# Attention step: the image columns and the image corner of the weights turned by TensorE, the image part of the weighted sum as one 153-column product a group, set-up fills in another order

## What is computed

```python
attn = jnp.einsum('bhnd,bhmd->bhnm', q, k) * attn_scale
attn, a_scale = fq_act(attn)              # to 8 bits, one scale for all
attn = log_int_softmax(attn, a_scale)     # integer exp, sum, ratio, then 0 or a power of two
out = jnp.einsum('bhnm,bhmd->bhnd', attn, v)
```

## Time and profile before

| | us |
|---|---|
| median of 3 runs | 1046.6 (1045.37 to 1047.09) |
| the profiled execution, its own time | 1041.93 |
| its span, first to last instruction | 1040.1 |
| attention, of that span | about 355 to 775 |
| mean granted TensorE clock | 0.841 of 2.4 GHz |

### The profile page before, as it was taken

How to read it: one execution, slowest core, us unless ns; L and a number is a source line. 1 busy time by engine, 2 the same in 40 slices (tenths; PEclk the granted TensorE clock), 3 DMA queues, 4 the chain that set the end, 5 groups by cost and what they waited for, 6 DMA issues and landing times. The chain is left out here.

```text
span 1040.1 us, 22682 instructions
## 1 busy us (share of the span) xinstructions
PE 709.4 (68%) x5955; PEld 482.6 (46%) x5956; DVE 883.8 (85%) x2422; ACT 711.7 (68%) x1376; POOL 168.9 (16%) x274
## 2 busy tenths in 40 slices
PE   3872396747888366666776676666645385999997
PEld 3552144424555233433443343343323254989896
DVE  5898986888888889999999999999978864666766
ACT  0254364957888699888888989899955294445453
POOL 5851500006555000000000000000003530000000
PEclk9995598988999687788777778878756597999999
DMA  8000000001111111111111111111012004355452
GB/s 255 3 2 0 0 1 1 0 0 38 37 37 37 33 29 25 24 23 23 23 29 24 24 23 25 24 23 24 13 62 105 18 1 151 126 193 203 154 199 89
DMA packets 84272, 54.71 MB, mean 53 GB/s; under 512 B 53705, under 2 KB 83177, under 8 KB 83977
## 3 DMA queue, kind: packets, MB, share of 16 engines
q1 hardware_dynamic: 83208, 54.11, 17.1%
q0 software_dynamic: 1024, 0.13, 0.2%
HBM read 11.90 MB, written 3.76 MB: 15 GB/s over the span
## 5 line engine op out<-in xcount | busy, mean ns | idle before, releaser
L1358 DVE SCALAR_TENSOR_TENSOR expo<-expo,con,pow 128x153 f32<-128x153 f32 x480 | 146.1, 376 | 0.8 <-ACT expo L1267 0.8
L1141 PE MATMUL at_rem<-word,ident_half 128*128 128x459 f16 x160 | 66.0, 412 | 102.9 <-ACT expo L1267 102.1
L1267 ACT ACTIVATE expo<-at_rem,con 128x459 f32<-128x459 f32 x160 | 95.2, 639 | 14.2 <-PE at_rem L1142 13.5
L953 DVE TENSOR_REDUCE rs_ends<-rs_banks 128x770 f32 (+1 forms) x96 | 91.3, 960 | 14.5 <-PE rs_banks L924 12.8
L873 ACT ACTIVATE rs_banks<-rs_banks 128x770 f32<-128x770 f32 x96 | 76.2, 798 | 25.3 <-PE rs_banks L916 24.0
L1223 ACT ACTIVATE word<-at_banks 128x459 uint8<-128x459 f32 x160 | 80.9, 560 | 10.7 <-PE at_banks L779 10.6
L1401 DVE CUSTOM_DVE_ANT_0 weight_top<-weight_top,line 128x2448 uint16<-128x2448 uint16 x64 | 86.2, 1346 | 2.1 <-ACT line L1259 2.1
L1141 PEld LDWEIGHTS at_rem<-word,ident_half 128*128 128x128 f16 x160 | 15.7, 98 | 152.9 <-ACT expo L1267 148.3
L1259 ACT ACTIVATE line<-weight_top 128x1224 f32<-128x1224 f32 x64 | 74.0, 1158 | 15.2 <-DVE weight_top L1386 15.0
L774 PE MATMUL at_banks<-pick,row_top 128*128 128x459 bf16 x160 | 73.4, 459 | 11.0 <-ACT word L1223 4.0
L1907 ACT ACTIVATE qk<-e_p,b1s 128x153 f32<-128x153 f32 x192 | 58.7, 391 | 29.8 <-PE e_p L1868 28.5
(11 more groups left out here) (390 smaller groups left out, 2089.8 us busy)
## 6 DMA issues: line engine op xcount, KB each, us to landing
qk<-vt SPq DMA_DIRECT2D x64, 384.0 KB, 3.1
rs_kb<-qk SPq DMA_DIRECT2D x128, 28.7 KB, 1.9
kb<-qk SPq DMA_DIRECT2D x128, 28.7 KB, 1.9
patches<-in_patches SPq DMA_DIRECT2D x4, 768.0 KB, 10.0
vi<-vt SPq DMA_DIRECT2D x32, 96.0 KB, 2.0
out<-vi SPq DMA_DIRECT2D x32, 96.0 KB, 1.8
pj_w<-in_w SPq DMA_DIRECT2D x1, 2304.0 KB, 8.4
qb<-qk SPq DMA_DIRECT2D x128, 6.0 KB, 1.8
```

The costliest lines, as they stand in the source:

```text
L953: v.tensor_reduce(ends[:, :, n, 5 * b:5 * b + 5], banks[:, slot(u, b), :, 0:5 * W].rearrange("p i (t n) -> p i t n", n=W), AX, ALU.max).th ...
L1141: pe.matmul(out, identh[:, :], bank(word, b).bitcast(F16), start=True, stop=False)
L1267: act.activation(bank(ex, b), rem[:, (u + b) % 2, 0:3 * N], ACT.Square, scale=2.0 ** 24, bias=c(5)).then_inc(sq_done, 1)
L1358: ins = v.scalar_tensor_tensor(ex[:, t, :], ex[:, t, :], c(7), pw[:, t, :].bitcast(BF16), ALU.add, ALU.mult, accum_out=tot[:, t:t + 1])
```

## The change

The vector transpose of the corner and the two ACT gathers (`p_image`, `p_both`) go. Group 2 on PE now is: three 128 x 128 transposes of planes 12 to 14 as before; 12 transposes that each turn one text plane's 32 image columns straight into its 32 partitions of the output (L1168); 12 products with a 32 x 32 piece of the identity, that turn the corner block by block (L1174, written as f32 into spare columns of the same PSUM buffer). ACT evicts the turned image rows and corner side by side into a single piece `imT` of 153 columns a group of heads, so that `weighted` needs one product for each instead of two, and `pT_all` shrinks from 2316 to 2295 columns. Both halves of L1386 (L1392 in the new numbering) and the image shares on ACT now wait for all three groups of PE. At the start of the stage the fills of `row_top` and `zero` go from DVE to POOL, ahead of POOL's fill of `word`; ACT no longer waits for all set-up before it copies the first rows, and PE waits for it only before `remainder`.

```diff
-        pi, pk = sb("p_image", [P, H, 32], BF16), sb("p_both", [P, HT, 32], BF16)
-        pall = sb("pT_all", [P, H * N + HT * (P + 32)], BF16)
+        pall = sb("pT_all", [P, RT * N], BF16)
...
+        imT = pall[:, H * N:RT * N].rearrange("p (t n) -> p t n", n=N)
...
             def _(pool):
+                pool.memset(row_top[:, :, :], 0.0).then_inc(words_set, 1)
+                pool.memset(zero[:, :], 0.0).then_inc(words_set, 1)
                 pool.memset(word[:, :, :], WORD).then_inc(words_set, 1)
...
                 def remainder(n, u, which):
+                    if first(n, 1):
+                        pe.wait_ge(set_up, 3)
...
                 def turn(n, u, which):
-                        if g == GROUPS - 1:
-                            pe.wait_ge(pi_done, n + 1)
...
-                            src = high[:, t, 0:NT] if t < RT else pi[:, 4 * (t - RT):4 * (t - RT) + 4, :].rearrange("p j n -> p (j n)")
-                            mm = pe.transpose(pT[:, slot, j * P:(j + 1) * P], src, identb[:, :])
+                            if t < RT:
+                                mm = pe.transpose(pT[:, slot, j * P:(j + 1) * P], high[:, t, 0:NT], identb[:, :])
+                            else:
+                                for q in range(4):
+                                    mm = pe.transpose(pT[32 * q:32 * q + 32, slot, j * P:(j + 1) * P], high[:, 4 * (t - RT) + q, IW:N], identb[:, :])
+                        if g == GROUPS - 1:
+                            for t in range(HT):
+                                for j in range(4):
+                                    r = slice(32 * j, 32 * j + 32)
+                                    mm = pe.matmul(corner_at(slot)[r, 32 * t:32 * t + 32], high[:, H + t, IW:N], identb[:, r], start=True, stop=True, skip_group_check=True)
                         mm.then_inc(tr_done, 1)
...
-                        pe.matmul(po[p:p + 64, q:q + NT], lhs, piT[:, t, :], start=False, stop=False, skip_group_check=True)
-                        pe.matmul(po[p:p + 64, q + NT:q + N], lhs, pjT[:, t, ID:32], start=False, stop=False, skip_group_check=True)
+                        pe.matmul(po[p:p + 64, q:q + N], lhs, imT[:, t, :], start=False, stop=False, skip_group_check=True)
...
                 turn_tops(0)
-                pe.wait_ge(set_up, 4)
...
-                def corner(n):
-                    if not first(n, 1):
-                        act.wait_ge(tr_done, n * GROUPS)
-                        act.wait_ge(pk_done, n)
-                    act.wait_ge(i_done, n * 2 + 2)
-                    act.activation(pi[:, :, :].bitcast(I16), high[:, 0:H, IW:N].bitcast(I16), ACT.Copy).then_inc(pi_done, 1)
-                    rank(pk[:, :, :], high[:, H:RT, IW:N]).then_inc(pj_index, 1)
...
-                            rank(piT[:, :, :], slot[:, 3 * P:6 * P].rearrange("p (t n) -> p t n", n=P)).then_inc(ev_done, 1)
+                            rank(imT[:, :, 0:NT], slot[:, 3 * P:6 * P].rearrange("p (t n) -> p t n", n=P))
+                            rank(imT[:, :, NT:N], corner_high((u + g) % 2)[:, :, ID:32]).then_inc(ev_done, 1)
...
-                act.wait_ge(words_set, 1)
-                act.wait_ge(set_up, 4)
                 per_step = act.alloc_register("per_step")
                 act.load(per_step, con[0:1, 0:1].bitcast(I32))
+                act.wait_ge(words_set, 1)
                 keep_tops(0)
+                act.wait_ge(words_set, 3)
+                act.wait_ge(set_up, 3)
...
-                v.memset(row_top[:, :, :], 0.0).then_inc(set_up, 1)
-                v.memset(zero[:, :], 0.0).then_inc(set_up, 1)
+                v.sem_inc(set_up, 1)
...
-                            v.wait_ge(pj_index, nb)
+                            v.wait_ge(tr_done, nb * GROUPS)
                         for h, half in enumerate(halves):
-                            if not first(nb, 1):
-                                v.wait_ge(tr_done, nb * GROUPS - 1 + h)
...
-                        v.wait_ge(pj_index, nj + 1)
-                        if not first(nj, 1):
-                            v.wait_ge(pv_done, nj)
-                        v.transpose(pjT.rearrange("p t n -> p (t n)"), pk[:, :, :].rearrange("p t n -> p (t n)")).then_inc(pk_done, 1)
                         v.wait_ge(ev_done, nj * GROUPS + GROUPS)
-                        v.wait_ge(pk_done, nj + 1)
```

More of the change, by code:

```diff
@@ L1019, in attention @@
         vbs, zero = sb("v_image_row", [P, 2, HT * 4 * HD], BF16), sb("zero_column", [P, 2], BF16)
-        pi, pk = sb("p_image", [P, H, 32], BF16), sb("p_both", [P, HT, 32], BF16)
-        pall = sb("pT_all", [P, H * N + HT * (P + 32)], BF16)
+        pall = sb("pT_all", [P, RT * N], BF16)
         ptT = pall[:, 0:H * N].rearrange("p (h n) -> p h n", n=N)
-        piT = pall[:, H * N:H * N + HT * P].rearrange("p (t n) -> p t n", n=P)
-        pjT = pall[:, H * N + HT * P:H * N + HT * (P + 32)].rearrange("p (t n) -> p t n", n=32)
+        imT = pall[:, H * N:RT * N].rearrange("p (t n) -> p t n", n=N)
         high = top[:, :, :].bitcast(BF16).rearrange("p w (n two) -> p w n two", two=2)[:, :, :, 1]
@@ L1029, in attention, with corner_at, corner_high @@
         pT, po = k.ps("at_pT", [P, 2, 1024], BF16, st), k.ps("at_out", [P, 512], F32, st)
+        def corner_at(slot):
+            return pT[:, slot, 6 * P:6 * P + 2 * HT * 32].bitcast(F32)
+        def corner_high(slot):
+            return pT[:, slot, 6 * P:6 * P + 2 * HT * 32].rearrange("p (t n two) -> p t n two", t=HT, two=2)[:, :, :, 1]
         sem = lambda *names: (k.sem("at_" + y) for y in names)
@@ L1034, in attention @@
         ends_done = k.sem("at_ends_done")
-        pi_done, pj_index, pk_done, pj_done, tr_done, ev_done, pv_done, out_done = sem(
-            "pi_done", "pj_index", "pk_done", "pj_done", "tr_done", "ev_done", "pv_done", "out_done")
+        pj_done, tr_done, ev_done, pv_done, out_done = sem(
+            "pj_done", "tr_done", "ev_done", "pv_done", "out_done")
         pj_loaded, a_done = k.sem("pj_loaded"), k.sem("at_a_done")
@@ L1167, in weighted @@
                             pe.wait_ge(out_done, half)
+                        else:
+                            pe.wait_ge(words_set, 2)
                         pe.matmul(po[:, 0:1], identb[:, :], zero[:, 0:1], start=True, stop=False, skip_group_check=True)
@@ L1248, in both_shares @@
                     if not first(n, 1):
-                        act.wait_ge(pj_index, n)
+                        act.wait_ge(tr_done, n * GROUPS)
                     for t in range(H, RT):
@@ L1282, in body @@
                     if last is not None:
-                        corner(last[0])
                         ranks(last[0], last[1])
```

## The result

| | before | after |
|---|---|---|
| median | 1045.37 (7 runs) | 1042.02 (7 runs) |
| ratio, 95% interval | | 0.9963 [0.9951, 0.9976] |
| the profiled execution, its own time | 1041.93 | 1042.02 |
| attention in it, barrier to barrier | 420.01 | 414.92 |
| everything else in its span | 620.11 | 625.30 |

The account below looks back on a forecast made before the run. DVE's own order was taken to set the pace, with ACT's second `line` a floor just under it. Loop 2.3 - 1.3 = 1.0, start 1.9, end 0.6: 3.5 off 1046.6 gives 1043.1 on the median's scale; range 1038.5 to 1049.

Parts of the forecast that it names:

- The floor: DVE's second addition waits for ACT's second `line`, so it starts no earlier than 4.91 after the shares; 4.99 before.
- 28 steps x 0.08 = 2.3: Attention loop on DVE: dropping the 0.38 transpose gains 0.08 a step in 28 of 32 steps, 2.3 us.
- PE's group 2, the minus 1.3: Loop: group 2 takes 0.83 at 2.4 GHz, about 1.25 at 1.2; in 9 slow steps ACT is 0.15 late, 1.3 back.
- The rule on small matmuls: PE's group 2: some 60 cycles of overhead per matmul would make it 1.15 and cost the sum some 0.5; weighed, not taken.
- the 0.28 of the sum: PE's group 2: time taken for the 24 small products, in rounds of four, 0.18 for transposes and 0.10 for corner products.
- The start: 1.9: Start of attention: evictions finish earlier, DVE is last, POOL's added fills cost 0.35; `octave` moves from 364.84 to 362.93.
- The end: 0.6: Last step: first addition keeps 0.25 of the 0.38, last rounding about 0.3 earlier, fewer products 0.05; together 0.6.
- The whole 0.38 counts: Rival, loop on DVE: all 0.38 of the transpose is gained in 28 steps, 13.1 in all, 1033.5; chance 5%.
- The gain is eaten: Rival: low-clock delays in half the steps, or PE or POOL at the start, leave -1.5 to +1.5, say 1045.8; chance 20%.
- One by one: Rival: PE's small products run serially, group 2 is 0.8 longer at 2.4 GHz, 13 us lost in the loop, 1054.8; chance 13%.
- Its turning point: In the serial-products rival: the change turns slower once group 2 on PE takes more than about 1.5.
- What would show it: Profile signs: DVE idle 0.3 before second addition, step 12.48, DVE below 98%; wrong if ACT's third eviction waits over 0.5 for PE.

Follow-up runs that it names:

- no_floor: Changed kernel with one square instead of two between ACT's two `line`s, and the maximum of finished output ahead of DVE's first addition; 1030.03 (5 runs), ratio 0.9847.
- two_transposes: Changed kernel with two idle 128x96 block transposes per step put on DVE, each into a piece of its own; one run, 1041.38.
- one_piece: Changed kernel with 24 more small PE products, all into the first 32 partitions, ahead of the proper ones that overwrite them; one run, 1054.19.

## Why the prediction was right, and where not

**The floor.** Forecast: the second addition 4.91 after the start of the shares, 0.08 gained, not 0.38. Measured 4.92 (3.488 from the end of the first half; the floor by the earlier trace rows was 3.485), 0.078 gained. The room under it, 0.38 - 0.08 = 0.30, came out as 0.31. The runs with put-back holds and those without the floor show the cause.

**28 steps x 0.08 = 2.3** is too much: 31 steps gave 1.72. The 28 are each about 0.06 shorter, not 0.078, and the three ahead of them gave nothing. Of the missing 0.018, some 0.012 stand between the second addition and the first exponential, which start 1.192 apart in the changed kernel (1.181 before; 1.184 in no_floor). This goes with the wait: the distance is 1.191 or 1.192 in every kernel whose second addition waits for `line`, 1.180 to 1.184 in those where it doesn't (1.187 in two_transposes, where the idle time is used up), and the addition itself takes 1274 ns after and 1266 before. What in the wait does it was not tried. Step 12.48 was forecast, 12.50 came.

**PE's group 2, the minus 1.3,** is the term that was mis-sized most. The length: 0.83 forecast, 0.69 measured at 2.4 GHz; 1.25 forecast at 1.2 GHz, and 1.00 to 1.05 measured in the first image's group and the last three's, which are all but wholly at that level. The count was right: 9 steps in the lower level forecast, and 9 of the loop's groups begin in it. But the clock rises during the group (big transposes 0.107 apart, small ones 0.056), and the group takes 0.79 to 0.93. ACT's idle time before `line` in these nine steps falls to 0.07 to 0.21, and never to zero. Only behind the first image's group (1.05) was there none left, and `line` started 0.03 late. Nearly nothing was lost where 1.3 was subtracted. The two errors, 0.6 too much and 1.3 too little, made 1.0 of what was 1.72. That the sum's 3.5 stands near the whole kernel's 3.9 is therefore in part luck: attention itself gained 5.09, and all three parts were put too low.

**The rule on small matmuls.** The corner products into one piece follow each other after 25 ns at 2.4 GHz, which is 60 cycles of that clock, though they have 32 columns. The Trainium skill, "TensorEngine Tiling (Array Packing)", Instruction Overhead, gives each matmul about 60 cycles, and one piece behaves so. Four products into four pieces share one such slot, so the figure of the Trainium skill is per piece here, and the 0.28 of the sum (0.24 measured) was nearer than the 0.6 by the rule.

**The start: 1.9, measured 2.21.** That DVE would be last and `octave` lose its 2.16 of idle time was right. Its 0.35 for POOL's added fills was too much: the set-up ended 7.46 after the barrier (7.54 before) and not 7.79. `octave_step` (L1315) slipped in behind the first short fill with 0.25, and the cast behind it stood 1.83, until POOL's long fill ended. This is the branch that the rule of the Trainium skill, "SBUF — State Buffer", Who interferes with whom, allowed: who issues first has the shared pair for a whole instruction. With it the forecast was 2.0.

**The end: 0.6, measured 1.17.** These parts are read from the two timelines; no run tried them apart. The additions' 0.25 came (0.24). The rounding's 0.3 was 0.58: from group 1 on, four evictions follow on each other without a wait for PE, 1.81 in one piece. Products and copy behind it gave 0.03. The last 0.32 was in no term. Behind the last maximum the barrier opens after 0.43, before after 0.75. In the records POOL lets 0.397 pass between its two semaphore instructions of this barrier in the kernel before, 0.078 in the changed one and at every other barrier of both. The longer pause is there in all three profiles with the old start and in none of the eleven with the new one, so it goes with the start's edits; how is open.

**`weighted`** with a product less for each group: nothing forecast, nothing seen. In the last step, where nothing covers it, it takes 1.10 from first start to last end, 1.12 before.

**The rivals.** *The whole 0.38 counts* fell by the floor; without the floor a hold does count in full (0.16 of 0.16). *The gain is eaten* by the lower clock did not occur. *One by one* did not occur, but its price was about right: 13 us forecast in the loop for 0.8 more of group 2; 10.0 measured with 0.80 more. Its turning point was not. With group 2 at 1.49 and more the kernel is already 0.71% slower. By the idle times of the changed kernel the sum of max(0, d - idle) eats 5.1 us at d = 0.51, so the change turns slower once group 2 takes about 1.2 and not 1.5; this is worked out, not run.

**What would show it.** Idle time of 0.3 put to `line` in nearly every step was half right: the time is there, but split, 0.16 ahead of the first addition and 0.16 ahead of the second (3.488 to 3.327 when the second wait fell, 3.172 when both did), and between 400 and 700 us its releaser is named only once. The starts show it, the list of waits does not. Two other signs misled. DVE's busy share of the loop was to fall below 98% and fell only to 98.48. And one sign of being wrong came: ACT waits for PE before its third eviction longer than 0.5 (0.52 to 0.77) in 7 of the 32 steps. In the loop it cost nothing, since idle time before `line` was left; the sign was set too low.

## What to carry to other kernels

Before work is taken from the busiest engine, add up for each of its later waits how early the awaited thing could be there: the smallest of these margins caps the gain, and here the remedy was to reorder the other engine (one square instead of two between the lines), which was worth 10 us where the removed work was worth 2. A wait that only the saving opens up is not there in the profile before, and hardly shows in the one after. And where stages are parted by barriers, compare the stage and not the run: others' noise was twice the effect.

## What the runs showed of the hardware

- A 128x96 block transpose of 0.27 on DVE delays the start of the next instruction by 0.20 if that doesn't wait for it, by 0.31 if it waits for it alone, and by 0.38 if it waits for ACT as well; in this last case one of the two waits stands in the trace as an instruction of its own.
- Transposes and products with 32 output partitions start 1 to 6 ns apart into different 32-partition pieces, and 56 ns (128 columns) or 25 ns (32 columns) apart into the same, at 2.4 GHz. By the records, those into idle pieces start ahead of earlier ones into a busy piece (one_piece). ACT's eviction starts 0.09 behind the end of the last of them (0.07 at 1.2 GHz), an end that the profile models.
- DVE takes an addition 0.18 behind the end of ACT's `line` in every kernel here where it waits for it.
- POOL passed one barrier 0.32 later in the kernels where it had one fill to do in that stage than in those where it had three.
